# Two attentions whose softmax denominators are summed by GpSimd: one addition per unit goes to an accumulating transfer, and TensorE sums two parts instead of three

## The reference, cut to what matters

```python
attn = softmax(sim)                       # over the 1024 keys
out  = einsum('bhij,bhdj->bhdi', attn, v)
...
weights = softmax((qk + qe) / sqrt(d_head), axis=-1)
output  = einsum('bhqk,bhkd->bhqd', weights, v)
```

## Time and profile before

| | |
|---|---|
| median of three runs | 2824.72 us |
| profiled execution, its own time | 2824.42 us |
| its span | 2822.6 us |
| PE busy | 2467.3 us, 87% |
| DVE busy | 1989.9 us, 70% |
| POOL busy | 1967.6 us, 70% |
| ACT busy | 1403.2 us, 50% |

### The profile page before, as it was taken

How to read it: one execution, slowest core, us unless ns; L and a number is a source line. 1 busy time by engine, 2 the same in 40 slices (tenths; PEclk the granted TensorE clock), 3 DMA queues, 4 the chain that set the end, 5 groups by cost and what they waited for, 6 DMA issues and landing times. The chain is left out here.

```text
span 2822.6 us, 47289 instructions
## 1 busy us (share of the span) xinstructions
PE 2467.3 (87%) x18516; PEld 822.8 (29%) x18516; DVE 1989.9 (70%) x3075; ACT 1403.2 (50%) x2548; POOL 1967.6 (70%) x763
## 2 busy tenths in 40 slices
PE   7799999999999999968998999999999999660355
PEld 2464222222222222225552222222222222240234
DVE  4475778778778778627886878788787878278234
ACT  3344555555555655623335666666566666450112
POOL 3123888888888888844445888888888888740773
PEclk9899999999999999989999999999999999885657
DMA  4994222232221232029764233222322231170347
GB/s 80 235 239 146 50 50 50 54 80 60 51 52 50 50 80 64 9 101 278 247 228 142 50 92 70 65 49 72 98 58 64 50 85 29 61 224 0 93 129 257
DMA packets 236268, 278.16 MB, mean 99 GB/s; under 512 B 65393, under 2 KB 171377, under 8 KB 232843
## 3 DMA queue, kind: packets, MB, share of 16 engines
q1 hardware_dynamic: 225548, 249.89, 32.6%
q0 software_dynamic: 6144, 16.85, 1.9%
q10 hardware_dynamic: 4352, 8.39, 0.8%
HBM read 165.17 MB, written 110.67 MB: 98 GB/s over the span
## 5 line engine op out<-in xcount | busy, mean ns | idle before, releaser
L854 POOL TENSOR_TENSOR room_af<-room_af 128x2048 f32<-128x2048 f32 x160 | 725.5, 4535 | 164.2 <-ACT room_af L826 150.4
L1225 POOL TENSOR_TENSOR bias<-bias 128x2048 f32<-128x2048 f32 x160 | 724.6, 4529 | 133.2 <-ACT bias L1195 114.4
L826 ACT ACTIVATE room_af<-PS 128x512 f32<-128x512 f32 x1024 | 555.9, 594 | 396.7 <-PE PS L748 396.7
L635 DVE CUSTOM_DVE_ANT_0 PS<-PS,bias 128x1024 f32<-128x1024 f32 x512 | 620.0, 1241 | 163.1 <-PE PS L623 143.1
L1195 ACT ACTIVATE bias<-PS 128x512 f32<-128x512 f32 x1024 | 555.7, 594 | 356.0 <-PE PS L1123 354.6
L1004 DVE TENSOR_REDUCE row_min_kf<-PS 128x1 f32<-128x1024 f32 x512 | 603.7, 1219 | 120.4 <-PE PS L996 115.5
L741 PE MATMUL PS<-QS_af,KS_af 128*128 128x512 f16 x1024 | 334.5, 387 | 14.3 <-PEq L90 4.5
L1118 PE MATMUL PS<-stacks_kf 128*128 128x512 f16 x1024 | 334.9, 387 | 12.6 <-PEq L90 8.5
L774 PE MATMUL PS<-room_af,V_af 128*32 128x512 f32 x2048 | 273.2, 605 | 1.2 <-ACT room_af L826 1.2
L1143 PE MATMUL PS<-bias,V_kf 128*32 128x512 f32 x2048 | 272.7, 605 | 1.2 <-ACT bias L1195 1.2
L748 PE MATMUL PS<-turned_bias,eyes 64*32 64x512 f16 x4096 | 210.6, 388 | 0.0
(11 more groups left out here) (184 smaller groups left out, 2973.4 us busy)
## 6 DMA issues: line engine op xcount, KB each, us to landing
query_key_halves<-bias SPq DMA_DIRECT2D x32, 768.0 KB, 4.0
query_key_halves<-room_af SPq DMA_DIRECT2D x32, 512.0 KB, 4.3
stacks_kf<-query_key_halves SPq DMA_DIRECT2D x64, 256.0 KB, 7.9
KS_af<-query_key_halves SPq DMA_DIRECT2D x48, 256.0 KB, 4.9
QS_af<-query_key_halves SPq DMA_DIRECT2D x48, 256.0 KB, 6.9
lows_kf<-query_key_halves SPq DMA_DIRECT2D x96, 128.0 KB
token_rows<-rows_t SPq DMA_DIRECT2D x16, 514.0 KB, 4.3
FT_t<-token_rows SPq DMA_DIRECT2D x16, 514.0 KB, 5.6
```

The source lines that it names most:

```text
L635: nc.vector.tensor_tensor_reduce(out=max_ps[n % len(max_ps)], in0=max_ps[n % len(max_ps)], in1=bias_h[:, g * HG + j, z:z + N], scale=-1.0, ...
L826: nc.scalar.activation(prob[:, n % PR, head, :], score_ps[s % 3], ACT.Exp).then_inc(exps, 1)
L854: nc.gpsimd.tensor_tensor(acc[:, u % 2], so_far, prob[:, n % PR], ALU.add).then_inc(acc_ok, 1)
L1225: nc.gpsimd.tensor_tensor(acc[:, u % 2], so_far, prob[:, n % PR], ALU.add).then_inc(acc_ok, 1)
```

## The change

In both attentions:

- Tile 0 of a unit is no longer written into the ring but into `sums[u % 2]`. The ring (`ring`, `PR` = 6) holds tiles 1 to 7 of each unit in turn (`STEPS` = 7). In the first attention `sums` and the single `acc` lie in the unused half of the table's memory, `zf`; in the second `sums` is a new tile.
- Tile 1 is added to `sums` by a transfer from SBUF to SBUF that accumulates (`move_tile`, `dma_start(..., accum_op=ALU.add)`), issued from POOL's queue, 128 rows of 8 KB.
- POOL adds tiles 2 to 6 into `acc` by four additions and then `acc` into `sums` by a fifth (`add_sums`).
- PE sums two parts, tile 7 and `sums`, in place of three. In the last unit it sums four: `sums`, tiles 7 and 6, and `acc`, so that POOL makes only three additions there.
- The denominator stands in step 3 of the next unit (`DEN` = 3), the reciprocals in steps 4 to 7. In the first attention `EARLY` and `LATE` are written anew: step 3 has the one product, steps 5 and 7 have three.
- POOL's `finish` comes one unit later (`BACK` = 2) in step 2, and in the first attention the store likewise.
- ACT waits for the transfer of tile 1 before it writes tile 7 of the same unit, which takes the same ring slot.

Core of the diff (first attention; the second has the same `prob`, `move_tile`, `add_tile`, `add_sums`, the same waits of ACT and the same loop on POOL):

```diff
-                PR = 4
+                PR = 6
...
-                ADDS = KTU - 3
+                MOVED = 1
+                ADDS = KTU - 2 - MOVED
+                STEPS = KTU - 1
+                FIN, BACK = 2, 2
+                def prob(n):
+                    u, kt = divmod(n, KTU)
+                    return sums[:, u % 2] if kt == 0 else ring[:, (u * STEPS + kt - 1) % PR]
...
-                EARLY = ((), (1,), (), (), (), (), (11,), ())
-                LATE = ((0,), (2, 3), (4, 5), (6,), (7, 8), (9, 10), (12, 13), (14, 15))
-                DEN = 1
+                EARLY = ((), (1,), (), (), (), (), (), (13,))
+                LATE = ((0,), (2, 3), (4, 5), (6, 7), (8, 9), (10,), (11, 12), (14, 15))
+                DEN = 3
...
-                                pe.wait_ge(acc_ok, ADDS * (u + 1))
-                                parts = [prob[:, (KTU * u + kt) % PR] for kt in range(ADDS + 1, KTU)] + [acc[:, u % 2]]
+                                if u < NU - 1:
+                                    pe.wait_ge(acc_ok, ADDS * (u + 1))
+                                    parts = [prob(KTU * u + KTU - 1), sums[:, u % 2]]
+                                else:
+                                    pe.wait_ge(moved, 16 * MOVED * (u + 1))
+                                    pe.wait_ge(acc_ok, ADDS * (u + 1) - 2)
+                                    parts = [sums[:, u % 2], prob(KTU * u + KTU - 1), prob(KTU * u + KTU - 2), acc]
...
+                                if kt >= 1 and j == 0 and u * STEPS + kt - 1 >= PR:
+                                    u, kt = divmod(u * STEPS + kt - 1 - PR, STEPS)
+                                    act.wait_ge(weighed, KTU * u + kt + 2)
+                                    if kt < MOVED:
+                                        act.wait_ge(moved, 16 * (MOVED * u + kt + 1))
+                                    elif kt < STEPS - 1:
+                                        act.wait_ge(acc_ok, ADDS * u + max(kt - MOVED, 1))
+                                    else:
+                                        act.wait_ge(max_full, job_at[(u, "den")] + 1)
...
+                            def move_tile(n):
+                                u, kt = divmod(n, KTU)
+                                pool.wait_ge(exps, HG * (n + 1))
+                                if kt == 1:
+                                    pool.wait_ge(weighed, KTU * u + 1)
+                                if MOVED * u + kt >= 2:
+                                    pool.wait_ge(moved, 16 * (MOVED * u + kt - 1))
+                                nc.gpsimd.dma_start(sums[:, u % 2].rearrange("p j n -> p (j n)"), prob(n).rearrange("p j n -> p (j n)"),
+                                                    accum_op=ALU.add).then_inc(moved, 16)
...
+                            def add_sums(u):
+                                pool.wait_ge(moved, 16 * MOVED * (u + 1))
+                                pool.wait_ge(acc_ok, ADDS * (u + 1) - 1)
+                                nc.gpsimd.tensor_tensor(sums[:, u % 2], sums[:, u % 2], acc, ALU.add).then_inc(acc_ok, 1)
...
                             for n in range(NU * KTU):
-                                add_tile(n)
-                                if n % KTU == ADDS and n >= KTU:
-                                    finish(n // KTU - 1)
-                            finish(NU - 1)
+                                u, kt = divmod(n, KTU)
+                                if kt == 0 and u >= 1:
+                                    add_sums(u - 1)
+                                if kt == 1:
+                                    move_tile(n)
+                                if kt == FIN and u >= BACK:
+                                    finish(u - BACK)
+                                if MOVED + 2 <= kt < KTU - (1 if u < NU - 1 else 2):
+                                    add_tile(n)
+                            for u in range(NU - BACK, NU):
+                                finish(u)
```

More of the change, by code:

```diff
@@ L1231, in _, with add_sums @@
-                            finish(NU - 1)
+                                if done >= 1:
+                                    pool.wait_ge(acc_ok, done)
+                                nc.gpsimd.tensor_tensor(acc, prob(n - 1) if first else acc, prob(n), ALU.add).then_inc(acc_ok, 1)
+                            def add_sums(u):
+                                pool.wait_ge(moved, 16 * MOVED * (u + 1))
+                                pool.wait_ge(acc_ok, ADDS * (u + 1) - 1)
+                                nc.gpsimd.tensor_tensor(sums[:, u % 2], sums[:, u % 2], acc, ALU.add).then_inc(acc_ok, 1)
```

134 lines of the change are left out of this document (78 added, 56 removed).

## The result

| | before | after |
|---|---|---|
| median on the same chip | 2823.41 us (4 runs, 2821.93 to 2827.25) | 2778.45 us (4 runs, 2776.12 to 2779.80) |
| profiled execution, its span | 2824.42, 2822.6 us | 2776.12, 2774.3 us |

The ratio is 0.9829, 95% interval 0.9818 to 0.9841: 45 us less. Forecast were 53.2 us and 2771 us; the time lies inside the likeliest case's own range of 2760 to 2784.

The account below looks back on a forecast made before the run. PE was taken to set the pace, with DVE close behind in the first attention. Second attention 26.7, first 22.9 and end 3.6 us sum to 53.2; 2824.4 less that gives 2771 us, range 2756 to 2815.

Parts of the forecast that it names:

- the likeliest case's own range: Whole kernel: the forecast of 2771 us, given chance 0.62, was expected within 2760 to 2784 us.
- PE, 0.86 us a unit: Denominator on PE: 8 fewer matmuls save 0.86 us per unit, 26.7 us per attention if PE is the bound throughout.
- DVE's idle time before its copy: Sign on DVE: its idle time before its copy should be 0.86 us less.
- First attention, 0.12 us taken off: First attention: 0.12 us lost to DVE with three products in steps 5 and 7, leaving 0.74 us per unit, 22.9 us.
- The issue: POOL: issuing the transfer was to cost 1.04 us, bounds zero and four times that, with POOL still waiting in both attentions.
- By a hair: Second attention: PE's denominator does not wait for POOL's sum, which ends 1.1 us before it is wanted.
- The transfer: Accumulating transfer of tile 1: lands in 10.6 us, bounds 4.0 to 19.4, hidden within 14.2 us (second attention) or 17.8 (first).
- landings under 14 us: Sign for the transfer: no wait of ACT for it, and every landing under 14 us.
- The end: End of the second attention: last denominator ends at 2442.6 instead of about 2446.2 us, 3.6 us gained.
- Half gain: Rival, chance 0.20: DVE takes back half in steps 4 to 7, 2794 us; also counts ACT and POOL serialising, 2798 us.
- Late landing: Rival, chance 0.09: ACT stalls before tile 7; 2885 us at landing time L = 19.4, slower than before from about 17.6.
- Dear issue: Rival, chance 0.06: issue of 4.1 us makes POOL's round exceed the unit, 2864 us; decides from about 3.4 us.

Follow-up runs that it names:

- e2: Kernel before, with PE summing two parts instead of three (tile 6 left out of the denominator), nothing moved: 2782.74 us, ratio 0.9800.
- e3: Changed kernel with a third part put back on PE (tile 7 summed twice) in all units but the last: 2838.07 us, ratio 0.9996.
- e8: Changed kernel with the old EARLY and LATE tables in the first attention, denominator still in step 3: 2820.19 us, ratio 0.9968.
- e7: Changed kernel with an extra POOL operation of 2.37 us ahead of each join but the last: 2835.17 us, ratio 1.0033.
- e5: Changed kernel with a ring of 5 tiles instead of 6 in both attentions: 2783.31 us, ratio 0.9842.
- e6: Changed kernel with a ring of 4 tiles instead of 6: 2829.73 us, ratio 1.0004.
- e11: Kernel before, run once more with nothing changed: 2827.30 us, one execution.
- e1: Changed kernel, run once more with nothing altered: 2786.96 us, ratio 0.9816 to the kernel before.
- e4: Changed kernel with the transfer moving 16 columns in place of 2048: ratio 0.9818, three executions of 2787.01 to 2790.18 us, a fourth 4248.53 us.
- e9: Changed kernel with a second accumulating transfer for tile 2, PE summing one part, ring of 7 in the first attention: 3007.82 us, ratio 1.0647.
- e12: Changed kernel with PE summing one part in the first attention only, its two transfers placed away from the maxima rows: 2770.64 us, ratio 0.9792.

## Why the prediction was right, and where it was off

**PE, 0.86 us a unit.** Right, and shown three ways: the denominator's step fell from 5.83 to 4.97 us, e2 gives it without the rest, and e3 takes it back. DVE's idle time before its copy fell nearly by the 0.86 us that the prediction wanted: by 0.7 us a unit in the second attention (2.7 to 2.0) and 0.8 in the first. Second attention 28.18 us, as forecast.

**First attention, 0.12 us taken off.** Right to 0.1 us: 29.53 us against 29.6. The new tables cost 0.05 us against e2's unit of 29.48, DVE took nothing more, so the 0.12 us were a size too large and not a missing term. The steps that were freed of a reciprocal are 2 and 3, not 1 and 2 as the prediction says; nothing hung on it. What I didn't see is how much hung on the tables (e8, 1.4 us).

**POOL.** The issue was put at 1.04 us; it takes 0.87, of which 0.61 delay what follows; the multiplication behind it takes another 0.3 us longer. The join was to end 10.7 us into the next unit in the second attention and ended 10.6 us in (2005.88 for a unit from 1995.3); 8.3 us in the first, where it was 8.0 (707.26, unit from 699.31). "By a hair" was right too: the margin of 1.1 us was about 0.8, as e7's 2.37 us cost 1.6.

**The transfer.** Put at 10.6 us from twice a plain load; the median was 8.5 and 8.7 us and the longest 14.7 us, inside the bounds of 4.0 to 19.4. One of the prediction's signs, landings under 14 us, was missed without harm: the 14.7 us belong to the first unit, whose transfer was issued 8.1 us into it and not 10.6. Of the others the longest took 13.6 us, 0.6 us under the 14.2 after which the ring was to stall. So this margin too was thin, and only e5 and e6 show it. The Trainium skill, page "Collectives: The Full Stack", section "The bandwidth ceiling: the fold count and why AG ≠ RS ≠ AR", explains with two source reads per addition why a ReduceScatter between cores has half the bandwidth of an AllGather. For this transfer inside one core the trace agrees only loosely: the medians are 1.6 times the 5.3 us of a plain load, and the least, 6.9 us, is 1.3 times that. No run here separates a second read from other causes.

**The end.** 3.6 us forecast, 3.4 us measured.

**The sum.** 53.2 us were forecast and 45 came, while every term of the sum came out within a few us: the sum had no term for the stages outside the units. From the profiles, the units gave 25.0 + 26.9 = 51.9 us over 31 units each (I had 49.6), the end 3.4. But the start was 1.9 us longer, the stretch between 2.1, and the last stage, its 3.4 us at the beginning aside, 2.9: together 6.9 us back, so 48.3 between the spans. The remaining 3.3 us are the choice of executions: the profiled one of before was slower than its median, that of the change the fastest of four. e11 shows that the stretch between moves by 3.2 us in the unchanged kernel. For the start and the last stage it was not shown in that run, which gave them back to 0.3 us. But e1, the changed kernel again, has the start 4.7 us shorter, and on one chip, e1 to e4, the two range over 3.3 and 4.2 us with the same code there. On that chip the whole change gave 51.7 us, close to the forecast. So the 6.9 us look like scatter of the other stages; that they are nothing else is not shown.

**The rivals.** Half gain: no, DVE was not in the way. Late landing: it didn't occur, but e6 produced it, at equality with the kernel before where its slot was wanted two steps (6.5 us) sooner. From my threshold, L = 17.6 us for a stall in every unit, this isn't tested directly, since it struck in half the units. The formula for it also had no term for the clock, which falls when PE has to wait that long (e6, e9). Dear issue: my formula, a round of POOL longer than the unit, had it decide from 3.4 us of issue. e7 added 2.37 us, which is an issue of about 3.0 us all told, and was already slower than before. The formula was too kind: it left out that in the second attention PE's wait for the join comes first.

## What to carry to other kernels

Work moved to an idle queue was worth here what it took off the engine that paces, 0.86 us for 8 matmuls, as long as each new dependence kept its margin; write each margin down, for the next step of the same kind uses it up. Before a large transfer is put into a loop, look for the small ones whose landing something waits for, and place it so that it has landed before they are issued (e9 and e12: the first attention took 1001 us with the one place and 933 us with the other). A wait that leads back to its own start, as join to denominator to tile 3 to join, charges every unit for what goes beyond the loop's slack, which can be less than the slack of the engine alone (0.8 against 1.4 us in e7). And a stall of the engine that paces can cost more than its own length, since the granted clock may fall behind it.

## What the runs showed of the hardware

- An accumulating transfer of 1024 KB from SBUF to SBUF landed in 6.9 us at least, 8.5 to 8.7 in the median and 14.7 at most, beside loads. One of 16 columns landed in 2.0 us at least (e4).
- Its issue occupies POOL for 0.87 us, with 16 columns as with 2048, and the next instruction starts 0.57 to 0.61 us after it.
- It takes 5.2 us of all 16 DMA engines. Of four small transfers on SP's queue, the first issued 1.5 us before it, the last had landed only 3.4 us after the last issue (e9).
- After PE had stood idle for 3.3 us the granted clock was 0.50 for 6.8 us, and 8 matmuls took 1.94 us in place of 1.06 (e9).
- POOL's multiplication (`finish`, L854 and L1266) takes 1.56 to 1.58 us right behind an issue, where it took 1.28 us before; the rows show no wait. The one behind the last unit's addition again takes 1.28 us (2390.91), but in e12, where `finish` of the first attention follows the join, it takes 1.59. In e4, where the transfer has almost no bytes, it takes 1.57 too, so the bytes are not the cause; beyond that the cause is open. In e12 the large additions behind an issue take 4.85 to 4.88 us in place of 4.54.
